# Epsilon in a decoder's attention quotient: added to the floor once per batch, and inside the two comparing operations of each head pair

## The reference

```python
D_mat = jnp.exp(log_D - max_log_D)
C = qk * D_mat
normalizer = jnp.maximum(jnp.abs(C.sum(axis=-1, keepdims=True)), jnp.exp(-max_log_D))
h = jnp.einsum('hst,htd->hsd', C / (normalizer + EPS), vh)      # EPS = 1e-6
```

## Time and profile before

| | |
|---|---|
| median of 3 runs | 1654.29 us (1653.3 to 1654.54) |
| the profiled execution | 1652.59 us, its span 1650.8 us |
| TensorE (PE) busy | 1465.0 us, 89% of the span |
| VectorE (DVE) busy | 930.8 us, 56% |
| ScalarE (ACT) busy | 501.9 us, 30% |
| GpSimd (POOL) busy | 311.7 us, 19% |
| chain that ended last | PE 71%, DVE 17%, ACT 5%, issue 4% |

### The profile page before, as it was taken

The page is one execution under the profiler, slowest core; times in us unless marked ns, Lnnn a source line. Parts: engine busy times, 40 slices in busy tenths (PEclk is TensorE's granted clock), DMA queues, the critical chain, the costliest instruction groups (busy, mean ns, idle before and its releaser), DMA issues.

```text
span 1650.8 us, 29327 instructions
## 1 busy us (share of the span) xinstructions
PE 1465.0 (89%) x10876; PEld 1127.5 (68%) x10912; DVE 930.8 (56%) x2750; ACT 501.9 (30%) x1191; POOL 311.7 (19%) x399
## 2 busy tenths in 40 slices
PE   5679999898888712799999999999999999999994
PEld 2356556556556411788788787887888878888783
DVE  8667999999989889332423324233242333423364
ACT  4556676675755652001001010010100101001023
POOL 4012121121112200112121121211212112121135
PEclk9689999999999755899999999999999999999998
DMA  6203213122220270176776777767767687676796
GB/s 179 71 28 95 77 65 115 55 81 71 81 74 2 102 312 32 50 294 237 277 275 220 295 246 264 283 215 295 255 251 288 210 300 262 238 293 219 289 341 200
DMA packets 92576, 311.04 MB, mean 188 GB/s; under 512 B 42838, under 2 KB 46940, under 8 KB 83164
## 3 DMA queue, kind: packets, MB, share of 16 engines
q1 hardware_dynamic: 79260, 287.87, 47.6%
q0 software_dynamic: 13248, 22.29, 6.0%
HBM read 273.18 MB, written 36.96 MB: 188 GB/s over the span
## 4 chain that ended last, share of the span: by engine, by line
PE 71%; DVE 17%; ACT 5%; issue 4%; POOL 1%; DMA 1%; DVEq 0%; POOLq 0%; ACTq 0%
PE bank L1045 38%; PE banks L1059 15%; PE bank L670 5%; PE banks L1062 4%; DVE arena L1478 3%; PE banks L772 2%; DVE arena L1940 2%; DVE arena L1468 1%; PE bank L672 1%; ACT arena L1209 1%; PE banks L783 1%; ACT arena L1140 1%; DVE arena L1518 1%; PE banks L753 1%; PE bank L800 1%
## 5 line engine op out<-in xcount | busy, mean ns | idle before, releaser
L1412 ACT ACTIVATE arena<-bank 128x160 f32<-128x160 f32 x288 | 87.4, 304 | 870.6 <-PE bank L1045 868.7
L1045 PE MATMUL bank<-keep,arena 128*128 128x160 f32 x2304 | 320.0, 299 | 1.9 <-DVE arena L2144 1.9
L1045 PE MATMUL bank<-arena 128*128 128x160 f32 x2304 | 319.8, 301 | 0.9 <-issue 0.9
L1045 PEld LDWEIGHTS bank<-keep,arena 128*128 128x128 f32 x2304 | 315.4, 189 | 5.8 <-issue 3.2
L1045 PEld LDWEIGHTS bank<-arena 128*128 128x128 f32 x2304 | 316.0, 191 | 4.2 <-issue 4.2
L2144 DVE TENSOR_TENSOR arena<-arena,bank 128x160 f32<-128x160 f32 x256 | 82.2, 321 | 405.4 <-ACT arena L1412 352.8
L1059 PE MATMUL banks<-arena 128*128 128x512 f32 x576 | 252.4, 592 | 0.0
L2331 POOL DMA_INDIRECT acc_rows<-arena,keep x64 | 102.9, 1607 | 630.0 <-DVE arena L2089 611.9
L1059 PEld LDWEIGHTS banks<-arena 128*128 128x128 f32 x576 | 107.6, 190 | 122.5 <-issue 122.5
L2087 DVE TENSOR_SCALAR arena<-banks,keep 128x512 f32<-128x512 f32 x32 | 24.0, 750 | 189.1 <-PE banks L1062 185.4
L670 PE MATMUL bank<-arena 128*128 128x512 f32 x224 | 104.4, 608 | 6.5 <-DVE arena L1478 6.5
(11 more groups left out here) (293 smaller groups left out, 1787.0 us busy)
## 6 DMA issues: line engine op xcount, KB each, us to landing
arena<-in_wup SPq DMA_DIRECT2D x32, 4096.0 KB, 12.4
arena<-in_wdn SPq DMA_DIRECT2D x32, 2048.0 KB
arena<-in_aup SPq DMA_DIRECT2D x32, 512.0 KB, 11.6
arena<-in_xT SPq DMA_DIRECT2D x32, 256.0 KB, 2.9
arena<-in_kT SPq DMA_DIRECT2D x8, 1024.0 KB, 5.6
arena<-in_v SPq DMA_DIRECT2D x32, 256.0 KB, 6.4
x_rows<-arena SPq DMA_DIRECT2D x8, 1024.0 KB, 4.4
acc_rows<-arena SPq DMA_DIRECT2D x8, 1024.0 KB, 6.8
```

What stands on the lines that cost most here:

```text
L1045: m = pe.matmul(u[:, g * CAP:(g + 1) * CAP], w, xeT[e.slot][:, c, :], start=(c == 0), stop=(c == C - 1))
L1412: act.activation(sg[k], Ub[k][:, 0:CAP], ACT.Silu).then_inc(up_a(f"silu{j}"), 1)
```

## The change

Epsilon leaves the chain of `head_out`. It is added to the floor by one more ScalarE operation per batch (8 in all), which waits for the exponential that made the floor and stands ahead of `gates_f`. The first comparing operation takes (epsilon minus the sum) against the new floor, the second (the sum plus epsilon) against that, so that `den` holds max(|sum|, floor) + epsilon as before. The separate addition (32 in all) and the wait for it are gone. `head_out(b, 0)` waits for the new step `floor` in place of `en`.

```diff
-        ga_a = steps("gate_scalar", [..., "gcol", "en", "w", "F", "Fhi", "Fm", "Fmid"])
+        ga_a = steps("gate_scalar", [..., "gcol", "en", "w", "floor", "F", "Fhi", "Fm", "Fmid"])
...
-        ev_v = steps("ev_vector", [x for j in range(NP) for x in (f"neg{j}", f"den{j}", f"eps{j}", f"rec{j}", f"out{j}")])
+        ev_v = steps("ev_vector", [x for j in range(NP) for x in (f"neg{j}", f"den{j}", f"rec{j}", f"out{j}")])
...
                 act.activation(wcol, cols[:, :, 64:64 + NH], ACT.Exp).then_inc(ga_a("w"), 1)
+                act.wait_ge(*ga_a.at("en", b))
+                act.activation(en[b.slot], en[b.slot], ACT.Copy, bias=CELL_EPS).then_inc(ga_a("floor"), 1)
...
                 if j == 0:
-                    dve.wait_ge(*ga_a.at("en", b))
+                    dve.wait_ge(*ga_a.at("floor", b))
...
-                dve.scalar_tensor_tensor(den, pv[:, :, :, DH], -1.0, floor, ALU.mult, ALU.max).then_inc(ev_v(f"neg{j}"), 1)
+                dve.scalar_tensor_tensor(den, pv[:, :, :, DH], CELL_EPS, floor, ALU.subtract, ALU.max, reverse0=True)\
+                    .then_inc(ev_v(f"neg{j}"), 1)
                 dve.wait_ge(*ev_v.at(f"neg{j}", b))
-                dve.tensor_tensor(den, pv[:, :, :, DH], den, ALU.max).then_inc(ev_v(f"den{j}"), 1)
+                dve.scalar_tensor_tensor(den, pv[:, :, :, DH], CELL_EPS, den, ALU.add, ALU.max).then_inc(ev_v(f"den{j}"), 1)
                 dve.wait_ge(*ev_v.at(f"den{j}", b))
-                dve.tensor_scalar(den, den, CELL_EPS, None, ALU.add).then_inc(ev_v(f"eps{j}"), 1)
-                dve.wait_ge(*ev_v.at(f"eps{j}", b))
                 dve.reciprocal(den, den).then_inc(ev_v(f"rec{j}"), 1)
```

More of the change, by code:

```diff
@@ L357, in decoder_kernel @@
         ga_t = steps("gate_tensor", ["gates_k", "parts", "gates", "cols"])
-        ga_a = steps("gate_scalar", ["parts", "ig", "abs", "relu", "exp", "log", "hi", "m0", "mid", "gcol", "en", "w", "F", "Fhi", "Fm", "Fmid"])
+        ga_a = steps("gate_scalar", ["parts", "ig", "abs", "relu", "exp", "log", "hi", "m0", "mid", "gcol", "en", "w", "floor", "F", "Fhi", "Fm", "Fmid"])
         ga_v = steps("gate_vector", ["cum", "g", "max", "neg", "r1", "lo", "Fr", "Flo"])
```

## The result

The changed kernel took 1650.92 us (median of 12 runs, 1647.6 to 1652.95), the kernel before 1653.15 us (median of 12 runs, 1652.6 to 1654.94): a ratio of 0.9984, 95% interval 0.9976 to 0.9992, that is 2.7 us less, between 1.3 and 4.0 (the two medians alone are 2.2 us apart). Two later measurements of the same kernel gave 0.9985 (0.9976 to 0.9994) and 0.9983 (0.9974 to 0.9992). By the means of the runs the three differences are 2.8, 2.6 and 2.8 us; weighted together they give 2.7 us with a standard error of 0.2. The forecast was 3.7 us less, 1650.6 us in a range of 1648.7 to 1653.7. The sign was right, and by the ratio the change is 0.16%, a little under the 0.2% that was named as the edge, where the forecast lay a little beyond it.

A forecast was written before the change was run, and what follows sets the result against it. The pipeline was taken as bound by a chain passing between engines, the experts by TensorE. Saving 4.0 us less 0.3 us for the new operation took 1654.29 to 1650.6 us, range 1648.7 to 1653.7 (narrow range 1649.9 to 1651.4).

The forecast's parts named there:

- Which quotients are on the chain: In the pipeline's eight steps, 20 of 32 `head_out` quotients lie on the chain that ended last; the other twelve are covered.
- What the addition costs: In `head_out`, the separate epsilon addition takes 0.20 us on the chain; twenty of these save 4.0 us.
- the exchange: Second comparison in `head_out` changes to the two-operand form; taken at zero, bounds 0.7 us gained to none.
- Whether the gain gets through: Behind `head_out` 0, 2 and 3, the 0.2 us saved each time passes on, with no other wait filling in.
- The waits of 0.31, 0.46 and 0.36 us: TensorE's idle for free banks, its broadcast's for ScalarE's decays, VectorE's for ScalarE's signs; first two forecast 0.1 and near 0.26.
- What the new operation costs: ScalarE's epsilon addition to the floor delays the chain in batches 0 and 1 by 0.16 us each, 0.3 us together.
- The sum: Whole kernel: 4.0 us saved less 0.3 us cost gives 3.7 us less, 1650.6 us.
- What the pipeline ends earlier is kept: After the pipeline, last router, selection and experts follow serially, so the full gain reaches the end.
- Rival 1: TensorE's clock falls on later steps' retention take the gain back: four falls lose 4.8 us, 1655.4 us; slower 0.04.
- Rival 2: Behind `head_out` 3 a second wait absorbs the gain: five times 0.2 us stay, 1651.6 us; chance 0.15.
- rival 3: ScalarE's new operation delays the decays and TensorE in every batch: six more times 0.16 us, 1651.6 us; chance 0.05.
- Rival 4: The change misses its aim: a costly ScalarE table load, or the addition half hidden by read latencies, 1652.6 us; chance 0.04.

## Why the prediction was right, point by point

**Which quotients are on the chain: right.** The additions in one quotient at a time show all 20 and eleven of the 12 that are covered; quotient 3 of step 2 is a twenty-first when the clock leaves it. In steps 1 and 2 the clock at the start blurs the reading. So the step from the chain to the count, on which the sum rested, holds.

**What the addition costs: right.** 0.20 us each from the first comparison to the reciprocal, and the second comparison's new form takes 166 ns, the old one's time. The prediction let the rows decide, with 0.20 us in each place: 20 places give 4.0. Its reason for taking the exchange at zero holds too: the first comparison of 132 ns stands where the scan ahead of it still runs (378.32 us, the scan until 378.40), and the second never does. The Trainium skill's cycle row ("VectorE: DVE Perf Modes", the section on the TRN2 errata), by which the sum would have been 1.4 us, doesn't agree with these 0.20 us. The whole times agree with the timeline: each of the three intervals alone reaches just below 1.4 (1.3, 1.0 and 1.3), but the three together, 2.7 us with an error of 0.2, don't.

**Whether the gain gets through: right, but for one place.** The waits of 0.31, 0.46 and 0.36 us moved by the gain, to 0.11 (in the steps other than 5), 0.25 and 0.56, and none ran out. In step 5, however, quotient 0 starts 0.36 us behind the statistics, idle for nothing the profile shows. The same place in the kernel before, in the changed kernel, and with the additions in quotient 1:

```profile
349.26 0.38 DVE L1491 BATCH_NORM_AGGREGATE arena<-arena 128x2 f32<-128x6 f32 x4
349.64 0.17 DVE L1552 SCALAR_TENSOR_TENSOR arena<-banks,arena 128x8 f32<-128x8 f32 x1
```

```profile
348.36 0.38 DVE L1493 BATCH_NORM_AGGREGATE arena<-arena 128x2 f32<-128x6 f32 x4
349.10 0.17 DVE L1554 SCALAR_TENSOR_TENSOR arena<-banks,arena 128x8 f32<-128x8 f32 x1 [0.36 <-issue]
```

```profile
347.41 0.38 DVE L1493 BATCH_NORM_AGGREGATE arena<-arena 128x2 f32<-128x6 f32 x4
347.80 0.17 DVE L1554 SCALAR_TENSOR_TENSOR arena<-banks,arena 128x8 f32<-128x8 f32 x1
```

It stands in every profile of the changed kernel and of the versions without and with a later floor, and in none of the kernel before, of the new operation alone or of the four with more additions. In the chain the semaphore waits of `head_out` are seen there one behind the other, which elsewhere lie beside the statistics. What makes VectorE late with them at this one place isn't shown; it goes with the program, since each program that has several profiles has it in all of them or in none. It takes 0.35 us.

**What the new operation costs: the mechanism was right, the sum too small.** In batches 0 and 1 it is 0.20 us, where 0.16 was taken, and "so I count nothing" for batch 7 was wrong by 0.10. That gives 0.5 us for 0.3, if all of it is kept. The runs say 1.2 (standard error 0.25) against the version without it, and 0.8 by itself. What makes the difference stays open. The clock changes near batches 0 and 1 in every profile, and it can make such a delay larger (by 0.2 us in the operation alone) or smaller (to 0.05 us in the pair without falls); whether it adds up to the 1.2 isn't shown.

**The sum.** Of 4.0 less 0.3, the traces leave: the quotients 4.0, less 0.35 for step 5, less 0.5 for the new operation, is 3.2. Measured are 2.7, with an error of 0.2, so the forecast's 3.7 is too large clear of the noise: the mechanism was right and the size a third too large. The prediction's own narrow range doesn't follow from its terms at the upper end either: the worst bounds of the exchange and of the floor give 1650.8 us, not 1651.4. The step of the prediction that had no term for the rest is the sentence "What the pipeline ends earlier is kept". In all three profiles of the changed kernel, and in both with the operation moved back, the last router runs L858 at the low clock: L865 starts 4.1 to 4.5 us after it in the changed kernel's three, where it is 2.9 in both profiles of the kernel before and in that with the new operation alone, a loss of 1.2 to 1.6 us. But one of two profiles without the new operation has 2.9 as well, and so have two of the four with more additions, so the change doesn't force it. Whether the changed kernel meets this fall more often than the kernel before is likely by these counts and not shown. The second such place is the experts' start, where a sooner rise of the clock gave back 1.0 to 1.2 us in the third profile of the changed kernel against its first two.

**The rivals.** Rival 1, the clock, is what moved most around the change, and it moved both ways: the fall in step 3 that went gave back 1.1 us (the same fall costs 1.3 in the changed kernel's third profile), against the 1.2 that were estimated, and the one in the last router took it again. It didn't gather the four falls that would have made the kernel slower; the profiles have none to two in the retention. Rival 2 (the gain behind quotient 3 stays) and rival 3 (the floor costs in every batch) have fallen in the traces, though the whole times alone would not have excluded the third. Rival 4 has fallen with the 28 table loads and with the 0.20 us gained in full from the comparison to the reciprocal.

## What to carry to other kernels

Walk the chain that ended last through every repetition of a loop and count where an edited instruction is on it: 32 copies of the same five operations had 20 that counted, and adding a small known delay to one place at a time confirms the map where whole times are too blunt. An operation moved to an engine that is mostly idle is free only where nobody waits for what stands behind it in the queue, so put it after what is waited for. And compare profiles instruction by instruction before crediting a span to a change: here the clock moved 1 to 1.5 us at a time in an unchanged program.

## What was not expected of the hardware

- A fall of TensorE's clock from full to half costs by its place: 0.9 to 1.3 us in a step where it meets the eight retention matmuls (5.40 us for 3.71), 1.2 to 1.6 us in the last router, and nothing when it lies 4 us earlier, beside VectorE's taps. Between two executions of one program it moved from 194 to 190 us.
- TensorE's clock rises 2.8 to 6.0 us after the experts' first matmul, and the time from that matmul to the end is 972.5 to 972.9 us in the profiles where it rises within 3.7 us and 973.6 to 974.1 in the others.
- VectorE's waits at the head of `head_out` 0 cost nothing in 7 of 8 batches and 0.35 us in step 5 of some of the programs.
- ScalarE's addition out of SBUF and back takes 229 ns for 128x32, against 197 ns for the same size out of PSUM, and what stands behind it in the queue starts 0.20 us later.
